# Folding W1's first two tiles before C0: a reordered first third of a two-layer adapter kernel

## The chip, the cores and the metric

One core of a Trainium2 chip runs the whole program. The metric is the device time of one execution in microseconds (us), lower is better. TensorE does the matmuls, VectorE (DVE) and ScalarE (ACT) split operands and empty PSUM, GpSimd (POOL) helps, and SyncE (SP) issues nearly all transfers between HBM and SBUF.

## The reference, cut to what matters

x is 8 batches of 256 tokens of 1024 features. Two residual layers follow each other, each a linear layer with adapters (`cond`) whose result only feeds a second linear map (`ffn`).

```
# layer 0: x = x + ffn0(cond0(x))
base   = x @ W0.T                              # W0: 1024 x 1024
cond0  = base + 2 * sum_e gate_e * (x @ A0_e) @ B0_e      # top-2 gates of 8, language bias
ffn0   = top1(cond0 @ route_w.T) * (cond0 @ A0f_e) @ Bw_e # 8 experts of rank 16
# layer 1: x = x + ffn1(cond1(x))
cond1  = x @ W1.T + b1 + 2 * (x @ lora_A[slot]) @ lora_B[slot]
ffn1   = cond1 @ Wb.T + b_base + 2 * (top-2 gates)*(cond1 @ A1_e) @ B1_e
```

Because `cond` is linear in x and only feeds linear maps, the kernel multiplies weights with weights first and the tokens afterwards. Three such products stand in the stretch that changes:

- **C0** (1024 x 136) = W0 folded with R0, the concatenation of route_w and A0f; **D0** is B0 folded with R0.
- **M** (1024 x 1160) = W1 folded with F, the concatenation of W_router, A1 and Wb. M goes on into the seven products of a Strassen scheme for all tokens.
- **FE** = the slots' lora_B folded with F.

## The kernel before, in words

Every f32 operand is split into a high part (an fp32r copy by ACT) and a low part (the rest, by DVE, line 789 via `lo`), and a product is three matmuls: high by high, high by low, low by high (`three`, lines 1239 to 1241). So each loaded operand costs one pass of ACT, then one of DVE, before TensorE may read it. C0 is the exception: two matmuls per step with R0's two parts side by side, 272 columns wide (`c0_step`, line 1246).

Each engine runs its program in the order written by hand; waits are on semaphores. A DMA queue belongs to SP, which also runs in order: a wait in it holds every later load.

TensorE's order before the main loop over the batches:

1. C0 from eight row tiles of W0 (128 matmuls of 272 columns), D0's fold (24 of 136).
2. FE in three column chunks of 240, 460 and 460 columns (`fe_steps`, 24 matmuls each), with `small0` (the tokens of the first two tiles times C0, 24 matmuls of 272) and its gates' turns between them.
3. The eight tiles of M, rows s = 0 to 7 (`m_chunk`; per row 24 matmuls of 240 and 48 of 460 columns). Row s uses PSUM banks 0 to 2 or 5 to 7 by turns. Behind row 0 stand the four groups of `ffn0`.
4. In the last two rows the chunk order is mixed; the bias matmul (`bias_part`, line 1380) stands behind row 6's second chunk.
5. The main loop `slot`, eight batches, which the change does not touch.

SP's order before: R0 and W0's row tiles, B0, the eight slots' lora_B, F in five pieces, A0, x, then W1's rows one at a time into one landing place (`load_w1`, each waits until the previous one is split), and behind row 1 the stores of FE to HBM (`fe_hi_dram`, `fe_lo_dram`).

DVE's pieces that the text speaks of: `gates0` (top-2 gates, ends in `hg`), `top1` (ends in `wh`), `b_times(k)` (six products for the bias row), `x1_add`, and per row of M the empty-out of PSUM (the loop over `add_ident`, `w1_split`, `lo`, `sub`, `lo_right`).

Of the kernel before, what the change touches and what calls it, by code (L numbers as in the profile page):

```python
# [5 lines left out]
P = 128  # L6
# [18 lines left out]
def adaln_ffn(nc, xT, lang_ids, slot_ids, W0, R0, A0, B0, Bw, W1, b1, lora_As, lora_Bs, F0, F1, F2, b_base, B1, out):  # L25

    C0C = ER + E + RC
# [6 lines left out]
    with ctx:  # L36
# [14 lines left out]
        C0lo, C0raw = twin("C0lo", [P, K, C0C])  # L51
        BwThi = sb("BwThi", [P, D], F32R)
# [175 lines left out]
        def m_count(s, c):  # L228
            return 3 * s + c + 1 if s < LAST else 3 * LAST + 2 * c + s - LAST + 1
# [41 lines left out]
        def by_batch(t):  # L271
            return t[:, :].rearrange("p (b k r) -> p k b r", b=NB, k=K)

        def k_first(t):
            return t[:, :].rearrange("p (k b r) -> p k b r", b=NB, k=K)
# [32 lines left out]
        def _(sp):  # L308
# [3 lines left out]
            def load_r0(g):  # L312
                load(r0_part(R0raw, g), R0[:, g * KH:(g + 1) * KH, :], r0_in[g])

            def load_f(i):
                c, k0, k1 = F_PARTS[i]
                load(f_part(i, 2), (F0, F1, F2)[c][k0 // KH if c else 0], f_raw_in[i])
# [4 lines left out]
            load_r0(0)  # L322
            for h in range(2):
                half = slice(h * D // 2, (h + 1) * D // 2)
                load(w0raw[0][:, half], W0[0:P, half], w0_in[0] if h else w0_half_in)
            load(w0raw[1][:, :], W0[P:2 * P, :], w0_in[1])
            load_r0(1)
            for j in range(2, K):
                load(w0raw[j][:, :], W0[j * P:(j + 1) * P, :], w0_in[j])
            load(b0raw[:, :], B0, b0_in)  # L330
            sp.wait_ge(ids_in, 32)
            for b in range(NB):
                slot = sp.value_load(ids[0:1, NB + b:NB + b + 1], min_val=0, max_val=lora_Bs.shape[0] - 1)
                load(w1raw[:, b * P:(b + 1) * P], lora_Bs[bass.ds(slot, 1), :, :].rearrange("s p c -> p (s c)"), bs_in)
            load_f(0)
            load(a0_part(C0raw), A0, a0_in)
            load(x_raw0[:, 0:D], xT[0, :, 0:D], x0_in[0])
            load_f(1)
            load_f(2)
            load(x_raw0[:, D:2 * D], xT[0, :, D:2 * D], x0_in[1])  # L340
            load_f(3)
            load_f(4)
            sp.wait_ge(bs_hi, 1)
            sp.wait_ge(bs_lo, 1)
            load_w1(0)
            load(BwTraw[:, :], Bw, bw_in)
            load(bcol[:, :], b1, bcol_in)
            load(x_raw1[:, 0:D], xT[1, :, 0:D], x2_in[0])
            sp.wait_ge(w1_hi, 1)
            sp.wait_ge(w1_lo, 1)  # L350
            load_w1(1)
# [34 lines left out]
            sp.wait_ge(w1_hi, K)  # L386
            sp.wait_ge(w1_lo, K)
# [69 lines left out]
        def _(gp):  # L457
# [10 lines left out]
            for g in range(2):  # L468
                gp.wait_ge(c0_hi, g + 1)
                c0 = slice(4 * g, 4 * g + 4)  # L470
                gp.tensor_tensor(C0lo[:, c0, ER + E:C0C], c0_sums[g], C0hi[:, c0, ER + E:C0C].bitcast(F32),
                                 ALU.subtract).then_inc(c0_lo, 1)
# [49 lines left out]
        def _(act):  # L522
# [5 lines left out]
            def r0_split(g):  # L528
                hi_half(r0_in[g], 16, r0_part(R0Thi, g), r0_part(R0raw, g), r0_hi)

            def f_split(i):
                hi_half(f_raw_in[i], 16, f_part(i, 0), f_part(i, 2), f_hi)

            def x_first(half):
                hi_half(x0_in[half], 16, xT_first[0][half][:, :], x_raw0[:, half * D:(half + 1) * D], xT_hi)

            def w1_split(s):
                hi_half(w1_in, 16 * (s + 1), ws_hi[s % 2][:, :], w1raw, w1_hi)

            r0_split(0)  # L540
            for h in range(2):
                hi_half(w0_in[0] if h else w0_half_in, 16, half_of(w0s_hi[0], h), half_of(w0raw[0], h), w0_hi)
            hi_half(w0_in[1], 16, w0s_hi[1][:, :], w0raw[1][:, :], w0_hi)
            r0_split(1)
            for j in range(2, K):
                hi_half(w0_in[j], 16, w0s_hi[j][:, :], w0raw[j][:, :], w0_hi)
            hi_half(b0_in, 16, b0hi[:, :], b0raw[:, :], b0_hi)
            act.wait_ge(w0_used, 2)
            hi_half(bs_in, 16 * NB, k_first(ws_hi[1]), by_batch(w1raw), bs_hi)

            def c0_half_part(g):
                hi_half(c0_done, g + 1, c0_sums[g], banks[:, 4 * g:4 * g + 4, RC:2 * RC], c0_half)

            def c0_part(g):
                hi_half(c0_sum, g + 1, C0hi[:, 4 * g:4 * g + 4, ER + E:C0C], c0_sums[g], c0_hi)

            c0_half_part(0)
            f_split(0)
            c0_part(0)
            c0_half_part(1)  # L560
            hi_half(a0_in, 16, a0_part(C0hi), a0_part(C0raw), a0_hi)
            c0_part(1)
            x_first(0)
            act.wait_ge(d0w_done, 1)
            act.activation(D0hi[:, :], p0[:, 0:RC], ACT.Copy, scale=2.0).then_inc(d0w_hi, 1)
# [83 lines left out]
            f_split(1)  # L649
            f_split(2)  # L650
            exp0(0)
            keep_fe(0)
            f_split(3)
            hgT_part(0)
            x_first(1)
            f_split(4)
            w1_split(0)
            whT_part(0, 0)
            keep_fe(1)
            hi_half(bw_in, 16, BwThi[:, :], BwTraw[:, :], bw_hi)  # L660
            exp0(1)
            keep_fe(2)
            hgT_part(1)
            w1_split(1)
            whT_part(1, 1)
            act.wait_ge(w1_lo, 2)
            act.wait_ge(fe_stored, 32)

# [3 lines left out]
            for s in range(LAST):  # L672
                par, row, p = s % 2, M_ROWS[s], s // 2
                act.wait_ge(m_ident, s + 1)
# [111 lines left out]
        def _(dve):  # L786
# [10 lines left out]
            def r0_split(g):  # L797
                lo_in(r0_hi, g + 1, r0_part(R0Tlo, g), r0_part(R0raw, g), r0_part(R0Thi, g), r0_lo)

            def f_split(i):  # L800
                lo_in(f_hi, i + 1, f_part(i, 1), f_part(i, 2), f_part(i, 0), f_lo)

            def x_first(half):
                dve.wait_ge(xT_hi, half + 1)
                lo(xT_first[1][half][:, :], x_raw0[:, half * D:(half + 1) * D], xT_first[0][half][:, :]).then_inc(xT_lo, 1)

            def w1_split(s):
                dve.wait_ge(w1_hi, s + 1)
                lo(ws_lo[s % 2][:, :], w1raw, ws_hi[s % 2][:, :]).then_inc(w1_lo, 1)
# [6 lines left out]
            r0_split(0)  # L816
            for h in range(2):
                lo_in(w0_hi, h + 1, half_of(w0s_lo[0], h), half_of(w0raw[0], h), half_of(w0s_hi[0], h), w0_lo)
            lo_in(w0_hi, 3, w0s_lo[1][:, :], w0raw[1][:, :], w0s_hi[1][:, :], w0_lo)
            r0_split(1)  # L820
            for j in range(2, K):
                lo_in(w0_hi, j + 2, w0s_lo[j][:, :], w0raw[j][:, :], w0s_hi[j][:, :], w0_lo)
# [786 lines left out]
```

## Time and profile before

| what | us |
|---|---|
| median of 3 runs | 466.69 (466.04 to 468.19) |
| the profiled execution's own time | 466.59 |
| its span in the profile, first to last instruction | 464.7 |
| TensorE busy in it | 447.0 (96%) |
| DVE busy | 306.9 (66%) |
| ACT busy | 151.0 (32%) |

Times in rows below are microseconds from the start of the span, so the execution's time is the span and 1.9 us around it. A timeline row gives start, duration, engine, line, operation, destination<-source, the shape, how many were merged, and in brackets how long the engine idled before it and what released it. Matmuls overlap, so a row's duration is longer than its distance to the next row; the distance is the pace. PEclk is the granted TensorE clock as a share of 2.4 GHz.

### The profile page before, as it was taken

What the parts mean: (1) busy time and instruction counts of PE and PEld (TensorE: products, weight loads), DVE (VectorE), ACT (ScalarE), POOL (GpSimd) and SP (SyncE); (2) the same over time, 40 slices, a digit from 0 to 9 for tenths busy, and PEclk for the clock granted to TensorE, in tenths of its full rate; (3) what the DMA queues carried; (4) which work ended last, traced back from release to release, by engine and by line L of the source; (5) the groups of instructions that cost most, each with busy time, mean ns of one, the idle gap of its engine ahead of it and who ended that gap; (6) DMA issues with size and microseconds to landing.
All of it is one profiled execution on the core that took longest, in us unless ns stands there. A gap on an engine that the chain in (4) does not pass through costs nothing.

```text
span 464.7 us, 7813 instructions
## 1 busy us (share of the span) xinstructions
PE 447.0 (96%) x2758; PEld 414.9 (89%) x2758; DVE 306.9 (66%) x911; ACT 151.0 (32%) x314; POOL 72.6 (16%) x62
## 2 busy tenths in 40 slices
PE   4988799999999999999999999999999999999997
PEld 4977799999988898889999999999999999999986
DVE  3897637574758688578557648738747755864852
ACT  4685212322222463234233224224323423321310
POOL 2040000000002412402402222120240230220110
PEclk9999899999999999999999999999999999999999
DMA  8993131111001101104103201211210310300302
GB/s 253 383 413 138 45 149 45 47 46 44 20 35 45 50 23 49 46 18 143 48 6 107 69 28 63 98 46 62 98 45 17 135 57 1 109 9 1 107 2 90
DMA packets 15151, 37.08 MB, mean 80 GB/s; under 512 B 2439, under 2 KB 7305, under 8 KB 15118
## 3 DMA queue, kind: packets, MB, share of 16 engines
q1 hardware_dynamic: 15022, 36.66, 22.7%
q8 instruction: 18, 0.29, 0.3%
q0 software_dynamic: 96, 0.00, 0.2%
q14 instruction: 15, 0.12, 0.1%
HBM read 27.07 MB, written 9.59 MB: 79 GB/s over the span
## 4 chain that ended last, share of the span: by engine, by line
PE 83%; DVE 12%; ACT 2%; issue 2%; DMA 1%; SPq 0%; DVEq 0%; ACTq 0%
PE banks L1239 25%; PE banks L1241 25%; PE banks L1240 25%; PE banks L1246 4%; DVE G L789 2%; DVE WbTlo L789 2%; PE banks L1471 2%; PE banks L1283 1%; DVE left L789 1%; DMA ws_lo_raw<-in_W_dram 1%; DVE ws_lo L789 1%; PE banks L1380 0%; DVE x_raw L973 0%; DVE G_raw L1086 0%; DVE w0s_lo L789 0%
## 5 line engine op out<-in xcount | busy, mean ns | idle before, releaser
L1239 PE MATMUL banks<-G,left 128*128 128x460 f32 x224 | 88.0, 393 | 0.0
L1240 PE MATMUL banks<-G,left 128*128 128x460 f32 x224 | 82.9, 370 | 0.0
L1241 PE MATMUL banks<-G,left 128*128 128x460 f32 x224 | 82.9, 370 | 0.0
L1239 PE MATMUL banks<-WbThi,ws_hi 128*128 128x460 f32 (+1 forms) x216 | 74.6, 345 | 4.3 <-DVE WbTlo L789 3.8
L474 POOL TENSOR_TENSOR xTlo<-x_raw,xThi 128x512 fp32r<-128x512 f32 x28 | 37.9, 1374 | 238.5 <-ACT xThi L572 114.6
L1241 PE MATMUL banks<-WbThi,ws_lo 128*128 128x460 f32 (+1 forms) x216 | 73.4, 340 | 0.0
L1240 PE MATMUL banks<-WbTlo,ws_hi 128*128 128x460 f32 (+1 forms) x216 | 73.1, 338 | 0.0
L526 ACT ACTIVATE left<-x_raw 128x512 fp32r<-128x512 f32 x64 | 38.7, 627 | 59.9 <-DVE x_raw L946 29.3
L1239 PEld LDWEIGHTS banks<-WbThi,ws_hi 128*128 128x128 f32 x216 | 40.6, 188 | 8.8 <-DVE WbTlo L789 4.9
L1239 PEld LDWEIGHTS banks<-G,left 128*128 128x128 f32 x224 | 42.4, 189 | 4.5 <-DVE wzTlo L789 0.3
L1241 PEld LDWEIGHTS banks<-G,left 128*128 128x128 f32 x224 | 42.1, 188 | 4.7
L1240 PEld LDWEIGHTS banks<-G,left 128*128 128x128 f32 x224 | 42.4, 189 | 2.6
L1240 PEld LDWEIGHTS banks<-WbTlo,ws_hi 128*128 128x128 f32 x216 | 40.8, 189 | 3.3
L1241 PEld LDWEIGHTS banks<-WbThi,ws_lo 128*128 128x128 f32 x216 | 40.7, 188 | 3.1
L946 DVE TENSOR_TENSOR x_raw<-banks,x_raw 128x512 f32<-128x512 f32 x32 | 22.1, 692 | 30.4 <-PE banks L1241 29.5
L977 DVE TENSOR_TENSOR ybuf<-banks,ybuf 128x460 f32<-128x460 f32 x48 | 29.6, 629 | 11.4 <-PE banks L1241 10.6
L1239 PE MATMUL banks<-Mdir,left 128*128 128x256 f32 x128 | 36.5, 285 | 0.2 <-DVE left L789 0.2
L474 POOL TENSOR_TENSOR left<-x_raw,left 128x512 fp32r<-128x512 f32 x16 | 20.7, 1312 | 98.8 <-DVE hg L858 74.0
L1240 PE MATMUL banks<-Mdir,left 128*128 128x256 f32 x128 | 35.9, 281 | 0.0
L1241 PE MATMUL banks<-Mdir,left 128*128 128x256 f32 x128 | 35.9, 281 | 0.0
L789 DVE SCALAR_TENSOR_TENSOR left<-x_raw,left 128x512 fp32r<-128x512 f32 x48 | 32.2, 686 | 2.7 <-ACT left L526 1.9
L1241 PE MATMUL banks<-C0hi,xTlo 128*128 128x272 f32 x112 | 32.3, 288 | 0.0
(178 smaller groups left out, 938.2 us busy)
## 6 DMA issues: line engine op xcount, KB each, us to landing
x_raw<-in_xT_dram SPq DMA_DIRECT2D x16, 512.0 KB, 3.8
out_dram<-ybuf SPq DMA_DIRECT2D x14, 512.0 KB, 2.7
x_raw<-in_W_dram SPq DMA_DIRECT2D x8, 512.0 KB, 3.3
WbTlo_raw<-in_F_dram SPq DMA_DIRECT2D x4, 920.0 KB, 12.8
w0s_lo_raw<-in_W_dram SPq DMA_DIRECT2D x6, 512.0 KB, 9.4
Fbuf<-fe_hi_dram SPq DMA_DIRECT2D x16, 64.0 KB
WbTlo_raw<-in_F_dram SPq DMA_DIRECT2D x1, 960.0 KB, 6.6
out_dram<-ybuf SPq DMA_DIRECT2D x3, 230.0 KB, 2.4
```

What stands on the lines that cost most here:

```text
L474: return gp.tensor_tensor(out_, a, b, ALU.subtract)
L526: act.activation(dst, src, ACT.Copy).then_inc(ready, 1)
L789: return dve.scalar_tensor_tensor(out=out_, in0=src, scalar=scale, in1=hi.bitcast(F32), op0=ALU.mult, op1=ALU.subtract)
L946: dve.tensor_tensor(raw_quarter(raw, g), by_half(bank), raw_quarter(raw, g), ALU.add).then_inc(x1_sum, 1)
L977: return dve.tensor_tensor(ybuf[tile][:, y0:y0 + n], bank, base, ALU.add).then_inc(ready, 1)
L1239: pe.matmul(out_, l[0], r[0], start=start, stop=False, **kw)
L1240: pe.matmul(out_, l[0], r[1], start=False, stop=False, **kw)
L1241: return pe.matmul(out_, l[1], r[0], start=False, stop=stop, **kw)
L1246: ins = pe.matmul(banks[:, k, 0:2 * RC], w, R0T[:, j, :], start=j == 0 and n == 0, stop=j == K - 1 and n == 1)
L1283: pe.transpose(dst, src, ident[:, :]).then_inc(done, 1)
L1471: pe.matmul(y, hsT[half][:, :], Fbuf[:, s], start=False, stop=True, skip_group_check=True)\
```

## The change

- TensorE's first work is sixteen transposes of the identity.
- It then folds rows 0 and 1 of M, from W1 pieces (five, `WF_PARTS`) and F pieces (eleven, `F_PARTS`) that SP loads first, in the order of use. FE and D0's fold follow.
- C0 comes after them. W0 is laid out in column tiles and streams through a ring of four buffers (`W0_RING`), so that each tile gives its own two column halves and finishes at once; SP loads a tile when its buffer is free. The sums are emptied in four pairs by ACT and DVE (POOL did the low part before).
- `small0`, the gates and the turns move in among rows 2 to 4 of M, `ffn0` into row 4, and DVE's `b_times` is spread otherwise. The slots' lora_B is laid out so that one DVE instruction splits it in place of eight.
- In SP's order the load of W1's row 3 stands behind the load of b_base, which waits for DVE's memset of `b_acc`.

SP, its list shown as it stands after:

```
+            load_wf(0)
+            load_f(0)
+            load_f(1)
+            load_wf(1)
+            load_wf(2)
+            load_wf(3)
+            load_f(2)
+            load_wf(4)
+            for i in range(3, 11):
+                load_f(i)
...
+            load(R0raw, R0, r0_in)
+            load_w0(0)
...
+            load_w1(2)
...
+            sp.wait_ge(m_done, m_count(0, 2))
+            load_w0(1)
+            sp.wait_ge(m_done, m_count(1, 2))
+            load_w0(2)
+            sp.wait_ge(fe_done, 3)
+            load_w0(3)
+            sp.wait_ge(d0w_done, 1)
+            load(BwTraw[:, :], Bw, bw_in)
+            sp.wait_ge(c0_used, 1)
+            load_w0(4)
             sp.wait_ge(fe_hi, 3)
             sp.wait_ge(fe_lo, 3)
             sp.dma_start(fe_hi_dram[0:P, :], fe_keep[0][:, :].bitcast(F32)).then_inc(fe_stored, 16)
             sp.dma_start(fe_lo_dram[0:P, :], fe_keep[1][:, :].bitcast(F32)).then_inc(fe_stored, 16)
+            for j in range(5, K):
+                sp.wait_ge(c0_used, j - 3)
+                load_w0(j)
             sp.wait_ge(acc_step, 1)
             load(b_acc[0:1, RC:MC], b_base.rearrange("(a o) -> a o", a=1), bbase_in)
-            for s in range(2, K):
-                sp.wait_ge(w1_hi, s)
-                sp.wait_ge(w1_lo, s)
+            for s in range(3, K):
+                sp.wait_ge(w1_hi, s - 2)
+                sp.wait_ge(w1_lo, s - 2)
                 load_w1(s)
```

ACT, from the last tile of W0 on:

```
+            w0_split(7)
+            act.wait_ge(c0_used, 5)
+            x_first(0)
+            c0_half_part(2)
+            w1_split(2)
+            c0_part(2)
+            c0_half_part(3)
+            c0_part(3)
+            act.wait_ge(c0_used, K - 1)
+            w1_split(3)
+            hi_half(bw_in, 16, BwThi[:, :], BwTraw[:, :], bw_hi)
+            act.wait_ge(fe_stored, 32)
+            x_first(1)
+            exp0(0)
+            hgT_part(0)
```

DVE, from the same place on:

```
+            x_first(0)
+            c0_add(2)
+            w1_split(2)
+            c0_part(2)
+            c0_add(3)
+            c0_part(3)
+            dve.wait_ge(fe_stored, 32)
+            dve.memset(b_acc[:, :], 0.0).then_inc(acc_step, 1)
+            w1_split(3)
+            lo_in(bw_hi, 1, BwTlo[:, :], BwTraw[:, :], BwThi[:, :], bw_lo)
+            x_first(1)
+            gates0(0, 0)
+            hgT_part(0)
...
+            b_times(0)
+            top1(0)
+            fold_rows(2)
+            whT_part(0, 0)
+            gates0(1, 0)
+            hgT_part(1)
+            b_times(1)
+            top1(1)
+            fold_rows(3)
+            whT_part(1, 1)
+            for g in range(2):
+                x1_add(0, g, x_raw0, X1W_FIRST[g])
+            b_times(2)
+            fold_rows(4)
...
+            fold_rows(5)
+            for k in range(6, K):
+                b_times(k)
```

TensorE:

```
+            pe.wait_ge(ident_ready, 1)
+            for _ in range(16):
+                pe.transpose(pt_h1, ident[:, :], ident[:, :])
+            pe.wait_ge(wf_lo, 1)
+            pe.wait_ge(f_lo, 1)
+            m_steps(0, 0, 0, 2)
...
+            for k in range(K):
+                pe.wait_ge(w0_lo, k + 1)
+                if k in (4, 6):
+                    pe.wait_ge(c0_sum, k // 2 - 1)
+                for j in range(K):
+                    for n, w in enumerate(split_of(W0_RING[k % 4][0], W0_RING[k % 4][1], j)):
+                        ins = pe.matmul(banks[:, C0_BANKS[k // 2] + k % 2, 0:2 * RC], w, R0T[:, j, :],
+                                        start=j == 0 and n == 0, stop=j == K - 1 and n == 1)
+                ins.then_inc(c0_used, 1)
+            pe.wait_ge(w1_lo, 1)
+            pe.wait_ge(fe_lo, 3)
+            m_chunk(0, 0)
             pe.wait_ge(a0_lo, 1)
+            pe.wait_ge(c0_lo, 4)
             pe.wait_ge(d0w_lo, 1)
             small0(0, first_tile(0), 1)
+            m_chunk(0, 1)
             pe.wait_ge(ident_ready, 1)
             turn_small(hg_ready, 1, pt_hg, hg[:, :], thg_done)
+            m_chunk(0, 2)
             add_lora0(0)
+            pe.wait_ge(w1_lo, 2)
+            m_chunk(1, 0)
             turn_small(wh_ready, 1, pt_wh, wh[:, :], twh_done)
             small0(1, first_tile(1), 2)
+            m_chunk(1, 1)
             turn_small(hg_ready, 2, pt_hg, hg[:, :], thg_done)
+            m_chunk(1, 2)
+            add_lora0(1)
...
+                if s == 4:
+                    turn_small(wh_ready, 2, pt_wh, wh[:, :], twh_done)
                 pe.wait_ge(m_lo, m_lo_at(s - 2, 3 + s % 2))
                 m_chunk(s % 2, 1)
+                if s == 4:
+                    pe.wait_ge(bw_lo, 1)
+                    pe.wait_ge(whT_lo, 2)
+                    ffn0(0, 0, X1W_FIRST[0])
+                    ffn0(0, 1, X1W_FIRST[1])
                 m_chunk(s % 2, 2)
```

`fold_rows(s)` is the old loop's body for one row: `add_ident`, `w1_split(s + 2)` where s > 1, and the empty-out. `wf_split`, `w0_split` and `c0_part` are the two-step splits (ACT high, DVE low) of the new pieces.

## Rows read from the trace of the kernel before

**Rows 1.** Windows: busy time of each engine, granted clock (PEclk), DMA share, GB/s.
```profile
7.06:12.04 4.98, 4.98 (x23) 4.98 (x23) 2.47 (x3) 2.78 (x3) 0.00 (x0) 1.00 0.95 324
13.31:25.47 12.16, 12.16 (x98) 12.15 (x97) 10.92 (x24) 8.17 (x8) 0.00 (x0) 1.00 1.07 384
30.00:35.00 5.00, 2.94 (x25) 2.78 (x24) 5.00 (x4) 3.88 (x4) 1.77 (x1) 1.00 1.02 417
45.00:50.00 5.00, 2.57 (x13) 2.02 (x13) 4.44 (x9) 1.32 (x2) 0.00 (x0) 1.00 0.00 0
50.00:55.00 5.00, 5.00 (x28) 4.90 (x27) 2.16 (x3) 1.67 (x3) 0.00 (x0) 0.66 0.33 105
59.00:61.00 2.00, 2.00 (x11) 1.76 (x10) 0.29 (x1) 1.22 (x2) 0.00 (x0) 1.00 1.01 411
```

**Rows 2.** TensorE's waits, 0 to 200 us: total, times, longest.
```profile
PE banks L1246 <- DVE ws_lo L789: 6.5, 1, 6.5
PE banks L1239 <- DVE WbTlo L789: 3.8, 3, 2.4
PE banks L1239 <- DVE D0lo L789: 2.1, 1, 2.1
```

**Rows 3.** TensorE's timeline: row 1 of M, row 2's start, the bias matmul.
```profile
72.21 0.27 PE L1239 MATMUL banks<-WbThi,ws_hi 128*128 128x240 f32 x1
...
74.91 0.37 PE L1239 MATMUL banks<-WbThi,ws_hi 128*128 128x460 f32 x1
...
84.98 0.27 PE L1239 MATMUL banks<-WbThi,ws_hi 128*128 128x240 f32 x1
...
147.12 0.50 PE L1380 MATMUL banks<-b_acc,ones 128*128 128x400 f32 x1
```

**Rows 4.** ACT's timeline: splits that begin when a load has landed.
```profile
3.70 0.66 ACT L526 ACTIVATE R0T<-R0T_raw 128x544 fp32r<-128x544 f32 x1 [1.69 <-DMA R0T_raw<-in_R_dram]
...
6.22 0.63 ACT L526 ACTIVATE ws_hi<-ws_lo_raw 128x512 fp32r<-128x512 f32 x1 [0.61 <-DMA ws_lo_raw<-in_W_dram]
...
9.79 0.66 ACT L526 ACTIVATE R0T<-R0T_raw 128x544 fp32r<-128x544 f32 x1 [1.25 <-DMA R0T_raw<-in_R_dram]
10.95 1.06 ACT L526 ACTIVATE w0s_hi<-w0s_lo_raw 128x1024 fp32r<-128x1024 f32 x1 [0.50 <-DMA w0s_lo_raw<-in_W_dram]
```

**Rows 5.** Transposes of gates (source view): duration min/median/max in ns.
```profile
L1283 PE MATMUL banks<-ident,hg x16: 270/272/328, 42.2 to 415.7; 128*128 128x128 f32 x16
```

**Rows 6.** DMA issues: KB each and median us from issue to landing.
```profile
x_raw<-in_W_dram SPq DMA_DIRECT2D x8, 512.0 KB, 3.3
```

**Rows 7.** DVE's timeline.
```profile
55.02 0.17 DVE L863 TENSOR_TENSOR lgc<-banks,bias 128x8 f32<-128x8 f32 x1 [1.44 <-PE banks L1241]
...
57.08 0.29 DVE L858 TENSOR_TENSOR hg<-banks,gc 128x128 f32<-128x128 f32 x1
...
61.91 0.17 DVE L914 COPY lgt<-banks 128x8 f32<-128x8 f32 x1 [2.18 <-PE banks L1241]
...
63.25 0.29 DVE L858 TENSOR_TENSOR wh<-banks,gt 128x128 f32<-128x128 f32 x1
...
65.36 1.02 DVE L1059 MEMSET b_acc<- 128x1160 f32 x1 [0.19 <-issue]
...
77.16 1.68 DVE L1071 SCALAR_TENSOR_TENSOR b_acc<-WbThi,bcol,b_acc 128x240 f32<-128x240 f32 x3
...
110.71 0.30 DVE L1082 TENSOR_TENSOR banks<-banks,ident 128x128 f32<-128x128 f32 x1 [5.81 <-PE banks L1241]
112.14 1.23 DVE L789 SCALAR_TENSOR_TENSOR ws_lo<-x_raw,ws_hi 128x1024 fp32r<-128x1024 f32 x1 [1.13 <-ACT ws_hi L526]
...
116.32 2.27 DVE L789 SCALAR_TENSOR_TENSOR G<-G_raw,G 128x460 fp32r<-128x460 f32 x4
```

**Rows 8.** SP's timeline: the load of b_base, then W1's rows.
```profile
66.41 0.32 SPq L310 DMA_DIRECT2D b_acc<-in_b_base_dram  x1
66.83 59.42 SPq L310 DMA_DIRECT2D x_raw<-in_W_dram  x6
```

More of the change, by code:

```diff
@@ L534, in x_first @@
             def x_first(half):
-                hi_half(x0_in[half], 16, xT_first[0][half][:, :], x_raw0[:, half * D:(half + 1) * D], xT_hi)
+                hi_half(x0_in[half], 16, xT_first[half][0][:, :], x_raw0[:, half * D:(half + 1) * D], xT_hi)
             def w1_split(s):
[L538 to L542, printed above, removed]
@@ L664, in _ @@
[L664 to L667, printed above, removed]
             def keep(out_, src, ready):
                 act.activation(out_, src, ACT.Copy).then_inc(ready, 1)
-            for s in range(LAST):
-                par, row, p = s % 2, M_ROWS[s], s // 2
+            wf_split(0)
+            f_split(0)
+            f_split(1)
+            wf_split(1)
+            wf_split(2)
+            wf_split(3)
+            f_split(2)
@@ new lines, in _ @@
+            wf_split(4)
+            for i in range(3, 11):
+                f_split(i)
+            hi_half(bs_in, 16 * NB, k_first(bs_hi_t), by_batch(bs_raw), bs_hi)
+            hi_half(r0_in, 16, R0Thi, R0raw, r0_hi)
+            act.wait_ge(bs_lo, 1)
+            w0_split(0)
+            hi_half(b0_in, 16, b0hi[:, :], b0raw[:, :], b0_hi)
+            hi_half(a0_in, 16, a0_part(C0hi), a0_part(C0raw), a0_hi)
+            act.wait_ge(m_ident, 1)
+            keep(direct(0, M_ROWS[0]), m_psum(0, 0), m_hi)
@@ new lines, in _ @@
+            keep_fe(0)
+            w0_split(2)
+            keep_fe(1)
+            keep_fe(2)
+            act.wait_ge(d0w_done, 1)
+            act.activation(D0hi[:, :], d0w, ACT.Copy, scale=2.0).then_inc(d0w_hi, 1)
+            w0_split(3)
+            c0_half_part(0)
+            w0_split(4)
+            c0_part(0)
+            w0_split(5)
+            c0_half_part(1)
+            w0_split(6)
+            c0_part(1)
+            w0_split(7)
+            act.wait_ge(c0_used, 5)
+            x_first(0)
@@ L1092, in lo_right, with fold_rows @@
                     ins.then_inc(ready, 1)
-            for s in range(LAST):
+            def fold_rows(s):
                 par, row, p = s % 2, M_ROWS[s], s // 2
                 add_ident(s)
-                w1_split(s + 2)
+                if s > 1:
+                    w1_split(s + 2)
                 dve.wait_ge(m_hi, m_hi_at(s, 1))
@@ L1115, in _ @@
                         lo_right(p, which, right_raw(p, which), g_lo)
-                for k in ((s,), (4, 5), (6, 7))[max(0, s - 3)]:
-                    b_times(k)
+            wf_split(0)
+            f_split(0)
+            f_split(1)
+            wf_split(1)
+            wf_split(2)
+            wf_split(3)
+            f_split(2)
+            wf_split(4)
+            for i in range(3, 11):
+                f_split(i)
+            lo_in(bs_hi, 1, k_first(bs_lo_t), by_batch(bs_raw), k_first(bs_hi_t), bs_lo)
@@ L1118, in _ @@
+            for g in range(2):
+                x1_add(0, g, x_raw0, X1W_FIRST[g])
+            b_times(2)
+            fold_rows(4)
+            for g in range(2, 4):
+                x1_add(0, g, x_raw0, X1W_FIRST[g])
+            for k in range(3, 6):
+                b_times(k)
+            fold_rows(5)
+            for k in range(6, K):
+                b_times(k)
             for s in (LAST, K - 1):
@@ L1312, in _, with first_tile, m_steps @@
-            pe.wait_ge(bs_lo, 1)
-            pe.wait_ge(f_lo, 1)
-            fe_steps(0, K)
+            def first_tile(t):
+                return lambda k: (rows(xT_first[t][0], k), rows(xT_first[t][1], k))
+            def m_steps(par, c, k0, k1):
+                for k in range(k0, k1):
+                    ins = three(m_psum(par, c), split_of(ws_hi[par], ws_lo[par], k),
+                                (Wb_of[c][0][:, k, :], Wb_of[c][1][:, k, :]), k == 0, k == K - 1)
+                if k1 == K:
+                    ins.then_inc(m_done, 1)
@@ new lines, in _ @@
+            pe.wait_ge(f_lo, 3)
+            m_steps(0, 0, 4, K)
+            pe.wait_ge(wf_lo, 5)
+            m_steps(1, 0, 4, K)
+            for k in range(0, K, 2):
+                pe.wait_ge(f_lo, 4 + k // 2)
+                for par in range(2):
+                    m_steps(par, 1, k, k + 2)
+            for k in range(0, K, 2):
+                pe.wait_ge(f_lo, 8 + k // 2)
+                m_steps(0, 2, k, k + 2)
+            m_chunk(1, 2)
+            pe.wait_ge(bs_lo, 1)
+            pe.wait_ge(m_lo, m_lo_at(0, 1))
@@ new lines, in _ @@
+            for c in range(3):
+                if c == 1:
+                    pe.wait_ge(m_lo, m_lo_at(0, 3))
+                for k in range(K):
+                    ins = three(m_psum(0, c), split_of(bs_hi_t, bs_lo_t, k),
+                                (Wb_of[c][0][:, k, :], Wb_of[c][1][:, k, :]), k == 0, k == K - 1)
+                ins.then_inc(fe_done, 1)
+            pe.wait_ge(b0_lo, 1)
+            pe.wait_ge(r0_lo, 1)
+            pe.wait_ge(m_lo, m_lo_at(1, 4))
+            for j in range(K):
+                ins = three(d0w, split_of(b0hi, b0lo, j), (R0Thi[:, j, :], R0Tlo[:, j, :]), j == 0, j == K - 1)
```

374 lines of the change are left out of this document (147 added, 227 removed).

## The prediction

> **What bounds the kernel now.** I read the windows first, to see where TensorE stands still or runs slowly; then its waits, for what ended them; then its timeline, for the pace of each kind of matmul; then the other engines' timelines and the DMA's, for the prices of what is moved. From 55 us on the windows show TensorE full, and the main loop is untouched, so the time changes by what reaches the bias matmul at 147.12 us [rows 3] sooner or later. Ahead of it TensorE stands still 6.5 us until the first operands are split, 2.1 us for the end of D0 and 3.8 us in three waits for F's low parts, the longest 2.4 us [rows 2]. Twice it is slow. In 7.06 to 12.04 us it began 22 matmuls of 272 columns (226 ns each; the window's 23 counts one cut off), later 96 in 12.16 us (127 ns) [rows 1]: half pace, although the profile writes a granted clock of 1.00 there. And after the 2.4 us wait the granted clock is 0.66 over 50 to 55 us, after 1.00 in the five before; at 1.2 GHz in part of it, that cost (1 - 0.66) x 5 = 1.7 us. The 2.1 us wait in 30 to 35 us was not followed by a fall [rows 1].
>
> So some 12 us of waiting and 4.7 us of slow clock (3.0 of its 6.0 us at the start, and 1.7) are what a better order could win. The question is what waits the new order has.
>
> **The change part by part.** Work for TensorE is the same but for the sixteen transposes. The paces: a row of M (72.21 to 84.98) takes 12.77 us, 2.70 for 24 matmuls of 240 columns (112 ns) and 10.07 for 48 of 460 (210 ns) [rows 3]; FE is one more such row; C0 and `small0` go at 127 ns.
>
> *Start.* The sixteen turns begin when the identity is there, near 1.6 us. At 0.27 us each as an upper bound [rows 5] they end by 6.0, at half that by 3.8. Landings I take from before by bytes: 0.28 MB in order at 3.70 us, 0.80 MB at 6.22, 1.61 at 9.79, 2.13 at 10.95 [rows 4]. The first F piece (0.38 MB with W1's first) so lands at 4.2; ACT 0.6, DVE 0.65, TensorE at 5.5 us, 1 us earlier than now. Until F's third piece is split it has 24 matmuls of 240 columns, about 200 ns each at half pace: done by 11. That third piece is the 1.77th MB, on hand at 10.15; ACT 1.0 and DVE 1.15 give 12.4 us. So TensorE waits over 1 us again, and whatever the turns save before it is swallowed here.
>
> *To the end of C0.* From 12.4: the other 24 of 240 (2.7), 96 of 460 (20.1), FE (12.8), D0 (24 at 112 ns, 2.7), five tiles of C0 (80 at 127 ns, 10.1): 60.9 us. The later F pieces arrive every 1.2 us and feed 2.5 us of matmuls each; the smaller pieces' extra issues on SP and extra passes cost nothing behind that. The slots' lora_B, R0, W0 tile 0, B0 and A0 land behind F by 27 us and are split by 29.5; FE needs them at 35: 5 us of cover, also if the strided split of lora_B takes twice its pass.
>
> *W0 tile 5.* SP issues it when tile 1 is used, at 54.9, but behind tile 4 (issued at 52.9) and FE's two stores of 0.59 MB. Tile 4 alone lands 3.3 us after issue [rows 6], at 56.2; 1.71 MB more at 411 GB/s [rows 1] make 4.2 us: 60.4. ACT 1.06, DVE 1.2: TensorE at 62.9. **A new stall of 2.0 us** (bounds: 0 if the tile passes the stores, 3.3 if the stores take twice their bytes' time). The last 48 matmuls of C0 end at 69.0. Before, the stores had no W0 behind them. Tile 4 itself is ready at 58.5, 0.3 us before its turn: hardly any cover. Emptying C0's earlier pairs hides behind the next tiles, and row 2's first chunk (2.7 us) hides the last pair from `small0`; that POOL gives its two passes to DVE costs DVE four short ones there.
>
> *The first gates.* `hg` needs `small0` and DVE. TensorE comes to its turn after 2.7 + 3.0 + 5.0 us, at 79.8. DVE and ACT empty C0's last pair (four passes of about 0.4 with the matmul's tail: 1.9) and set `b_acc` to zero (1.02 [rows 7]): 72.0. Only then may SP load b_base and, 0.42 us on [rows 8], W1's row 3; it lands 3.3 later [rows 6], at 75.7. In ACT's and DVE's order its split stands ahead of Bw's, x's second tile's and the gates: ACT 1.06, three DVE passes of 1.2 back to back (3.5) give 80.3, and `gates0` takes 2.35 (55.02 to the end of 57.08 [rows 7]). Ready at 82.9: **a new stall of 3.1 us**. Everything queued behind it on TensorE (rows 2 to 7) waits. Bounds: 1.8, if the row lands in 2.0 us, to 4.
>
> *The second `whT`.* From 83.1 TensorE has 5.0 + 0.3, row 3 with `small0` and small turns (12.8 + 3.0 + 0.6) and in row 4 two chunks and a turn (7.8): 112.7. DVE starts `top1(1)` when row 3 and `add_lora0(1)` end, at 105.0: 1.6 (61.91 to the end of 63.25), then all of `fold_rows(3)`, 7.9 (110.71 to the end of 116.32) [rows 7], then `whT_part`, 0.4: 114.9. **A new stall of 2.1 us** (1 to 3). Earlier the fold of a row had no turn behind it.
>
> *To the bias.* 24 matmuls of `ffn0` (2.8), 5.0, row 5 (12.8), 5.4 with 0.6 of the wait for the last `lo` that stands today too, 5.0: 146.7. DVE's last two `b_times` (3.2 each, from rows such as 77.16 [rows 7]) and the low parts of the last rows end near 145.9, so DVE covers by only 0.8 us: what delays it by more comes straight through. The gain with a full clock from 12.4 on is 147.12 - 146.7 = **0.4 us**.
>
> *Clock.* Two terms. At the start, now 6.0 us of matmuls run at half pace (6.48 to 12.5 us); 5.5 us of matmuls stand ahead of the wait for F's third piece, so 0.5 to 1 us more would run slowly behind it: +0.4 (bounds 0, and 2.4 if the 6.0 us count afresh from 12.4). Then the stalls: a wait of 2.4 us was followed by a fall that cost 1.7, one of 2.1 was not [rows 1, 2]. The 3.1 us one is beyond the first: +1.7. The two of 2.0 and 2.1 are nearest to the second: nothing, with 1.7 each as the other bound.
>
> A rule speaks against the turns. The row of before [rows 5] gives their length and cannot show what they do to the clock, as they stand singly there. The Trainium skill (TensorE: Matmul & The Clock Gate, Part 4: PE-mode transpose) says that the full clock does not engage for transposes. By that rule the +0.4 stands, as I take it; if turns do count, it goes, and the sum is 467.9 in place of 468.3. No run yet shows which.
>
> **Sum.** The profiled execution, 466.59 us, is 0.1 below the median. 466.59 - 0.4 + 0.4 + 1.7 = **468.3 us**.
>
> **Rivals.**
> 1. *The clock stays up in every stall.* For it: 2.1 us did not lower it. Against: 2.4 us did. 466.6 us.
> 2. *It falls at the 2.0 and 2.1 us stalls too.* For it: they are close to the one that did. 470.0 for one more fall, 471.7 for both.
> 3. *The slow start lasts 6.0 us afresh from 12.4.* For it: before, the pace rose after 6.0 unbroken us. Against: 5.5 us ran ahead. 468.3 + 2.0 = 470.3.
> 4. *The early loads run at full rate*: 0.28 MB at 3.70, then 411 GB/s, so F's third piece lands at 7.3 and TensorE never waits for it; the first burst at half pace ends near 10.3. That is 2.1 us off: 466.2. Against: before, only 1.33 MB came in the 6.1 us after 3.70 [rows 4], at 218 GB/s, with pieces of 2 KB per partition, and these are 1 to 2 KB. The Trainium skill (DMA: Bandwidth & Descriptors, Specifications) gives full rate from 512 B on, which would make this rival the forecast; the trace of before disagrees over its first 9 us.
> 5. *The first gates are not late* (the other side): W1's row 3 comes soon enough for `hg`. That takes away 3.1 us and the fall: 463.5. It decides once the chain from C0's end to `hg` (13.9 us) is 2.2 us shorter, for 468.3 - 2.2 - 1.7 = 464.4. For it: 3.3 us is a median, and DVE passes overlap a little. Against: three orders written by hand hold it (SP behind the memset, DVE behind C0, the gates behind three splits).
>
> **How the numbers follow.** Forecast 0.34 (467.3 to 469.3), rivals 0.15, 0.16, 0.10, 0.08, 0.17 in their order. What this kernel's measurement can tell from no change is about 0.5%, 2.3 us: 464.4 to 469.0. Faster: rival 5 and a third of rival 4, 0.20. Slower: rivals 2 and 3 and a third of the forecast, 0.37. Same: the rest, 0.43. The range leaves out about half of rival 5 below and the far half of the double fall above: 463.5 to 471.7.
>
> **What would show it.** Right: TensorE's first fold matmul near 5.5 us and a wait ended by F's third piece near 12; waits of about 2, 3 and 2 us before C0's sixth tile, the first `hg` turn and the first `ffn0`, at about 61, 80 and 113 us; a granted clock under 1.00 behind the second; the bias matmul near 148.4. Wrong: no wait at the `hg` turn, SP's load of W1's row 3 ahead of C0's end, or DVE's `b_times` holding the bias.

## The result and the profile after

| | before | after |
|---|---|---|
| median, us | 467.44 (466.04 to 468.20, 4 runs) | 473.85 (473.24 to 474.20, 4 runs) |
| profiled execution, us | 466.59 | 473.24 |
| its span, us | 464.7 | 471.4 |
| mean granted clock | 0.996 | 0.982 |

The ratio is 1.0139, 95% interval 1.0108 to 1.0170: the change makes the kernel 6.4 us slower. 468.3 was forecast, with a range up to 471.7. The bias matmul, which stood at 147.12 us [rows 3], now starts 6.3 us later, and behind it only 0.4 us more is lost (471.4 - 153.42 against 464.7 - 147.12), so all of it happens in the first third. TensorE's waits of the kernel after, 0 to 160 us, against [rows 2]:

```profile
PE banks L1342 <- DVE hg L901: 3.2, 1, 3.2
PE banks L1418 <- DVE ws_lo L843: 1.9, 1, 1.9
PE banks L1327 <- DVE whTlo L843: 1.9, 1, 1.9
PE banks L1327 <- DVE ws_lo L843: 1.8, 2, 1.3
PE banks L1372 <- POOL ident L489: 1.5, 1, 1.5
PE banks L1418 <- DVE w0s_lo L843: 1.0, 1, 1.0
PE banks L1327 <- DVE WbTlo L843: 0.9, 2, 0.6
```

The 6.5 us at the start, the 3.8 for F and the 2.1 for D0 are gone. In their place stand `hg` (3.2), W0's tile 5 (`ws_lo` at line 1418, 1.9), the second `whT` (1.9), W0's tile 4 (`w0s_lo`, 1.0) and short ones among the first pieces. They sum to 12.2 us, against 12.4 before; but the turns, 1.52 to 5.06 us, fill 3.5 us in which TensorE waited before, so 3.4 us more go by without a matmul of the work. The rest is in the windows (busy us of each engine, granted clock third from the end, then DMA share and GB/s):

```profile
5.00:10.00 5.00, 2.91 (x17) 2.44 (x17) 2.26 (x5) 1.87 (x4) 0.00 (x0) 0.82 0.85 292
10.00:15.00 5.00, 4.42 (x21) 4.17 (x21) 4.10 (x5) 4.14 (x5) 0.00 (x0) 0.50 1.03 416
15.00:20.00 5.00, 5.00 (x24) 4.79 (x23) 4.82 (x6) 4.19 (x5) 0.00 (x0) 0.66 1.02 364
...
60.00:65.00 5.00, 4.00 (x31) 3.63 (x29) 1.58 (x2) 1.75 (x3) 0.00 (x0) 1.00 1.03 415
65.00:70.00 5.00, 3.07 (x25) 3.00 (x25) 4.28 (x6) 4.67 (x8) 0.00 (x0) 1.00 0.18 70
...
85.00:90.00 5.00, 2.77 (x8) 2.50 (x9) 3.79 (x16) 0.57 (x2) 0.00 (x0) 0.67 0.06 20
...
120.00:125.00 5.00, 4.82 (x21) 4.54 (x22) 3.14 (x7) 0.00 (x0) 0.00 (x0) 0.66 0.00 0
```

The granted clock falls three times where it fell once before: from 8 to 18 us, behind `hg`, and behind the second `whT`. Behind W0's tile 5 (65 to 70 us) it stays at 1.00. TensorE's timeline shows the pace in each stretch (start, duration, line, output and inputs, the idle time before):

```profile
5.34 0.35 PE L1327 MATMUL banks<-WbThi,ws_hi 128*128 128x240 f32 x1 [0.29 <-DVE WbTlo L843]
5.53 0.28 PE L1328 MATMUL banks<-WbTlo,ws_hi 128*128 128x240 f32 x1
5.65 0.27 PE L1329 MATMUL banks<-WbThi,ws_lo 128*128 128x240 f32 x1
...
7.58 0.35 PE L1327 MATMUL banks<-WbThi,ws_hi 128*128 128x240 f32 x1 [1.32 <-DVE ws_lo L843]
...
12.60 0.54 PE L1327 MATMUL banks<-WbThi,ws_hi 128*128 128x240 f32 x1 [0.58 <-DVE WbTlo L843]
12.93 0.42 PE L1328 MATMUL banks<-WbTlo,ws_hi 128*128 128x240 f32 x1
13.14 0.41 PE L1329 MATMUL banks<-WbThi,ws_lo 128*128 128x240 f32 x1
...
87.22 0.45 PE L1342 MATMUL banks<-ident,hg 128*128 128x128 f32 x1 [3.18 <-DVE hg L901]
...
120.18 0.36 PE L1327 MATMUL banks<-whThi,BwThi 128*128 128x256 f32 x1 [1.91 <-DVE whTlo L843]
...
153.42 0.84 PE L1472 MATMUL banks<-b_acc,ones 128*128 128x400 f32 x2
```

The first fold matmuls start 0.11 to 0.12 us apart, which is the full pace of 112 ns; from the third F piece at 12.60 they start 0.21 us apart. The 24 matmuls behind that piece take 5.24 us, until 17.84, where 24 of 240 columns take 2.70 at the full clock. The loads of W0's tiles 4, 5 and 6 in 54 to 70 us (KB each, median us from issue to landing), and SP's order there:

```profile
ws_lo_raw<-in_W_dram SPq DMA_DIRECT2D x2, 512.0 KB, 6.4
...
w0s_lo_raw<-in_W_dram SPq DMA_DIRECT2D x1, 512.0 KB, 4.6
```

```profile
55.83 0.33 SPq L329 DMA_DIRECT2D w0s_lo_raw<-in_W_dram  x1
56.27 0.36 SPq L380 DMA_DIRECT2D fe_hi_dram<-fe_keep_hi  x1
56.67 0.43 SPq L381 DMA_DIRECT2D fe_lo_dram<-fe_keep_lo  x1
57.83 2.34 SPq L329 DMA_DIRECT2D ws_lo_raw<-in_W_dram  x2
...
76.38 0.30 SPq L329 DMA_DIRECT2D b_acc<-in_b_base_dram  x1
76.78 6.17 SPq L329 DMA_DIRECT2D x_raw<-in_W_dram  x2
```

Tile 4 takes 4.6 us where 3.3 was taken from [rows 6], tiles 5 and 6 take 6.4 in the median. W1's row 3 goes out at 76.78, behind the zeroing of `b_acc` (75.32 to 76.34), and ACT splits it at 80.23; the gates stand behind three splits on DVE, and `hg` is made at 86.79 to 87.08. That is the chain of 13.9 us as forecast, started later.

### The profile page after: what moved, and what is told of

Read it like the earlier page. It is cut to its first block, busy times and chain, and to the rows that moved or that the text cites. A ratio compares the mean times of both kernels' runs of the same rounds, so it can differ in the third digit from the quotient of the medians.

```text
span 471.4 us, 7865 instructions
## 1 busy us (share of the span) xinstructions
PE 453.6 (96%) x2774; PEld 420.8 (89%) x2774; DVE 308.6 (65%) x917; ACT 154.7 (33%) x325; POOL 67.5 (14%) x60
## 4 chain that ended last, share of the span: by engine, by line
PE 79%; DVE 12%; DMA 4%; ACT 2%; issue 2%; SPq 1%; DVEq 0%; ACTq 0%
PE banks L1327 25%; PE banks L1329 24%; PE banks L1328 24%; DVE G L843 3%; PE banks L1418 2%; PE banks L1563 2%; DMA ws_lo_raw<-in_W_dram 1%; DMA WbTlo_raw<-in_F_dram 1%; DVE ws_lo L843 1%; PE banks L1342 1%; ACT ws_hi L550 1%; DVE left L843 1%; DVE G_raw L1103 1%; DMA x_raw<-in_W_dram 1%; SPq L329 1%
## 5 line engine op out<-in xcount | busy, mean ns | idle before, releaser
L1329 PE MATMUL banks<-G,left 128*128 128x460 f32 x224 | 82.9, 370 | 0.0
L1327 PE MATMUL banks<-WbThi,ws_hi 128*128 128x460 f32 (+1 forms) x192 | 69.6, 362 | 3.1 <-DVE ws_lo L843 1.8
L1329 PE MATMUL banks<-WbThi,ws_lo 128*128 128x460 f32 (+1 forms) x192 | 67.7, 353 | 0.0
L1328 PE MATMUL banks<-WbTlo,ws_hi 128*128 128x460 f32 (+1 forms) x192 | 67.7, 353 | 0.0
L1327 PEld LDWEIGHTS banks<-WbThi,ws_hi 128*128 128x128 f32 x192 | 38.8, 202 | 7.1 <-issue 2.8
L1328 PEld LDWEIGHTS banks<-WbTlo,ws_hi 128*128 128x128 f32 x192 | 38.9, 202 | 2.9
L1329 PEld LDWEIGHTS banks<-WbThi,ws_lo 128*128 128x128 f32 x192 | 38.6, 201 | 2.8
```

What stands on the lines that cost most here:

```text
L1327: pe.matmul(out_, l[0], r[0], start=start, stop=False, **kw)
L1328: pe.matmul(out_, l[0], r[1], start=False, stop=False, **kw)
L1329: return pe.matmul(out_, l[1], r[0], start=False, stop=stop, **kw)
```

## The experiments

All are edits of the changed kernel. Ratios are against the kernel before, run beside them on the same chip; its median was 466.96 in the first four and 468.09 in the last four. The changed kernel was not run again beside them: its 473.85 stands beside 467.44, so a gain read as a difference of medians is uncertain by about 1 us.

The second to sixth edits leave the start as it is, and still it differs between the executions profiled: the first matmul of 460 columns, which stands right behind the 24 of F's third piece, starts at 17.84 us in the changed kernel and at 15.58 to 17.55 in those five. A part of each gain can come from there. In all four runs of the changed kernel the mean granted clock is 0.982; in the runs of the second to fourth edit it lies between 0.980 and 0.996, so the falls of the clock are not the same in every execution either.

**Without the sixteen turns.**

```diff
-            for _ in range(16):
-                pe.transpose(pt_h1, ident[:, :], ident[:, :])
```

> The changed kernel without its sixteen turns of the identity. It ran the first twelve fold matmuls 112 ns apart (full pace), fell to half pace near 8.2 us and stayed there until 17.9, which cost 2.5 us behind F's third piece at 12.6 us. Theory A: the turns raise the clock too early; matmuls then finish fast, TensorE stands idle between the loads, and the clock falls. Without turns the 24 early matmuls run 213 ns apart, fill the waits, and the pace rises about 6 us after the first of them, near 12: 2 to 2.5 us faster than the changed kernel, 471.5. Theory B: the turns do nothing to the clock, as the Trainium skill says (TensorE: Matmul & The Clock Gate, Part 4: PE-mode transpose); then the first matmuls run at 112 ns here too and the time stays at 473.8. Theory C: the slow spell comes from the waits for loads alone: first matmuls at 213 ns, rise again near 18, time within 0.5 us of 473.8.

Measured: 473.44 us (472.31 to 475.80, 4 runs), ratio 1.0154 (1.0108 to 1.0199); the same as with the turns. Its timeline tells what the turns do:

```profile
5.29 0.54 PE L1327 MATMUL banks<-WbThi,ws_hi 128*128 128x240 f32 x1 [5.29 <-DVE WbTlo L843]
...
14.35 0.34 PE L1329 MATMUL banks<-WbThi,ws_lo 128*128 128x240 f32 x1
14.52 0.27 PE L1327 MATMUL banks<-WbThi,ws_hi 128*128 128x240 f32 x1
14.63 0.28 PE L1328 MATMUL banks<-WbTlo,ws_hi 128*128 128x240 f32 x1
```

Without them the first 24 matmuls go at 0.21 us and the pace rises at 14.5, behind 9.2 us with two waits (the windows write a granted clock of 1.00 there, as they did at the start of the kernel before). With them it is full from the first fold matmul on in the changed kernel's profile; in four of the other seven profiles with turns it is full only from 6.1 to 6.5 us on, behind three to five matmuls at 0.21. So the turns do raise the clock, some 8 us sooner, and theory B is out. The gain is lost again in the waits before 12.6 us: here the first matmul of 460 columns starts at 16.54, 1.3 us sooner than with the turns. That is theory A's way and half its size; 0.6 of it goes into a longer wait for W0's tile 4 (1.62 against 1.00), and by the medians the time is the same, as C had it.

**W1's row 3 ahead of the wait for `b_acc`.**

```diff
+            sp.wait_ge(w1_hi, 1)
+            sp.wait_ge(w1_lo, 1)
+            load_w1(3)
             sp.wait_ge(acc_step, 1)
             load(b_acc[0:1, RC:MC], ...)
-            for s in range(3, K):
+            for s in range(4, K):
```

> SP's load of W1's row 3 put ahead of its wait for the memset of b_acc, nothing else. Theory A: the load by itself makes the first gates late. It lands about 4 us earlier (issued near 72.7 instead of 76.8 us), hg is there at 83, before TensorE's turn at 84; the wait of 3.2 us goes and with it the fall of the granted clock to 0.67 in 85 to 90 us, 1.7 us: 4.9 us faster, 469.0. Theory B: only the wait goes, and the slow spell comes from elsewhere: 3.2 us, 470.7. Theory C: the splits ahead of the gates move into C0's last emptying and the wait stays near 2 us: 1 to 2 us, 472.

Measured: 468.53 us (466.89 to 469.81, 10 runs), ratio 1.0031 (1.0014 to 1.0047). SP's timeline, then TensorE's waits:

```profile
71.86 0.33 SPq L329 DMA_DIRECT2D x_raw<-in_W_dram  x1
77.10 0.30 SPq L329 DMA_DIRECT2D b_acc<-in_b_base_dram  x1
```

```profile
PE banks L1330 <- DVE whTlo L846: 1.9, 1, 1.9
PE banks L1421 <- DVE ws_lo L846: 1.8, 1, 1.8
PE banks L1330 <- DVE ws_lo L846: 1.8, 1, 1.8
```

The row goes out 5 us ahead of b_base; no wait for `hg` stands among the longest or below them, and 5.3 us come back, where the wait of 3.2 and the fall behind it are 4.9: theory A, which gave 469.0. In this profile the second `whT` wait (1.91 us) has no fall behind it, and one of the same size, (0.24 + 0.10) x 5 = 1.7 us, stands behind W0's tile 5 (granted clock 0.76 in 65 to 70 us, 0.90 in 70 to 75); the two cancel.

**FE's stores behind W0's tiles 5 to 7.**

```diff
+            for j in range(5, K):
+                sp.wait_ge(c0_used, j - 3)
+                load_w0(j)
             sp.wait_ge(fe_hi, 3)
             ...
-            for j in range(5, K):
-                sp.wait_ge(c0_used, j - 3)
-                load_w0(j)
```

> The two stores of FE put behind the loads of W0's last tiles in SP's order, nothing else. Theory A: the stores hold tile 5 (1.9 us of wait) and slow tile 4 too (landing 4.6 us after its issue in place of 3.3, 1.0 us of wait): both waits go, 2.9 us faster, 470.9. Theory B: tile 4 is late because of the loads' own round trip (its buffer comes free only when tile 0 is used), the stores hold tile 5 alone: 1.9 us, 471.9. Theory C: both are bound by the ring of four buffers: within 0.5 us of 473.8.

Measured: 469.58 us (467.08 to 471.33, 10 runs), ratio 1.0051 (1.0025 to 1.0077); better than each theory gave. Its DMA view over 54 to 70 us:

```profile
ws_lo_raw<-in_W_dram SPq DMA_DIRECT2D x2, 512.0 KB, 4.3
...
w0s_lo_raw<-in_W_dram SPq DMA_DIRECT2D x1, 512.0 KB, 4.0
```

Tiles 5 and 6 take 4.3 us in place of 6.4, tile 4 takes 4.0 in place of 4.6. TensorE's wait for tile 4 shrinks to 0.4 us, the one for tile 5 to nothing, and `hg`'s is 2.8. That is 2.9 of the 4.3 us; the fold's first matmul of 460 columns also starts 0.85 sooner in this profile (16.99 against 17.84), which the edit doesn't touch. So the stores made both tiles late. Tile 4 was issued 0.44 us ahead of the first store in the changed kernel and still landed later for it; the 0.4 us left here are not the stores'.

**The second `whT` ahead of row 3's fold.**

```diff
-            fold_rows(3)
             whT_part(1, 1)
+            fold_rows(3)
```

ACT's half of it moves in the same way.

> whT_part(1, 1) put ahead of fold_rows(3) on DVE and ahead of row 3's part on ACT, nothing else. Theory A: the first ffn0 waits 1.9 us only because DVE empties a row of M first; that wait and the fall behind it (granted clock 0.66 in 120 to 125 us, 1.7 us) go: 3.6 us faster, 470.2. Theory B: the emptying of row 3, now begun 2.7 us later, makes a new wait in row 4 or 5 or at the bias matmul: 0 to 2 us faster. Theory C: a wait of 1.9 us does not lower the clock (one of 2.1 us did not in the kernel before), the fall has another cause: 1.9 us faster, 471.9.

Measured: 470.56 us (467.68 to 473.07, 10 runs), ratio 1.0072 (1.0043 to 1.0100): theory A. The windows have the granted clock at 1.00 where it was 0.66:

```profile
115.00:120.00 5.00, 5.00 (x31) 4.64 (x30) 4.72 (x9) 2.96 (x7) 0.00 (x0) 1.00 0.32 105
120.00:125.00 5.00, 5.00 (x26) 4.48 (x26) 5.00 (x11) 0.16 (x1) 0.00 (x0) 1.00 0.00 0
```

The wait is gone, and with it the fall: 3.3 us by the medians, where the wait of 1.91 and the fall of 1.7 are 3.6. The size is not settled by that. A part of theory B came too: the wait for `Mdir` in the last rows grows from 0.46 to 1.14 us. And in this profile the edit's gain is mixed with what it does not touch: the first matmul of 460 columns starts 1.8 us sooner (16.02), W0's tile 4 is waited for 0.7 us longer, and a fall stands behind tile 5 (0.66 in 65 to 70 us), where the changed kernel had none.

**All three edits together.**

> This kernel has all three of the single edits together: W1's row 3 loaded ahead of the wait on the first part of the carry, the fold's stores behind the loads of W0's tiles 5 to 7, and the second tile's wh split ahead of the copies of row 3. Each single edit gained against the changed kernel's 473.85 us: 5.3, 4.3 and 3.3. Theory A (three separate losses, so the gains add): 473.85 - 12.9 = 461.0 us, under the kernel before, with no wait of TensorE over 1 us between 50 and 140 us and the granted clock at 1.00 there. Theory B (a stall taken away early brings TensorE sooner to the next late operand, or a fall of the clock is shared by two of the stalls, so that the gains overlap): 464 to 466 us, with a wait left that none of the three singles shows. Theory C (SP, with the stores and row 3 moved, is late for the loads of W1's rows 4 and 5): 467 us or more.

Measured: 463.04 us (462.32 to 465.03, 6 runs), ratio 0.9902 (0.9871 to 0.9932): faster than the kernel before by 5 us, and 10.8 under the changed one where the singles sum to 12.9. Its waits up to 160 us:

```profile
PE banks L1329 <- DVE ws_lo L845: 2.1, 3, 1.3
PE banks L1374 <- POOL ident L492: 1.5, 1, 1.5
PE banks L1329 <- DVE Mdir L845: 1.1, 1, 1.1
PE banks L1329 <- DVE WbTlo L845: 1.0, 2, 0.7
PE banks L1420 <- DVE ws_lo L845: 0.4, 1, 0.4
```

The three stalls are gone, and the granted clock is 1.00 from 60 to 150 us. So A holds for the causes: three separate ones. One wait over 1 us is left against A's condition, 1.14 us for `Mdir`; it comes with the fold moved behind `whT` and was the same in that single. The size lies between A's 461.0 and B's 464 to 466. The profiles, one execution each, tell where the gap between 12.9 and 10.8 is not (us):

| | first matmul of 460 columns | bias matmul | between |
|---|---|---|---|
| changed kernel | 17.84 | 153.42 | 135.58 |
| row 3 early | 17.55 | 147.96 | 130.41 |
| stores late | 16.99 | 149.96 | 132.97 |
| `whT` first | 16.02 | 150.55 | 134.53 |
| all three | 17.16 | 142.80 | 125.64 |

Behind the start the singles gain 5.2, 2.6 and 1.1 us, 8.8 together, and the three edits 9.9, so there the gains do not overlap. Ahead of it the singles' profiles are 3.0 us sooner together and this one 0.7, which no edit made. C is out.

**TensorE kept busy while it waits for `hg`.**

```diff
+            for _ in range(24):
+                pe.transpose(pt_h1, ident[:, :], ident[:, :])
             turn_small(hg_ready, 1, pt_hg, hg[:, :], thg_done)
```

> The changed kernel with 24 turns of the identity ahead of the turn of hg, so that TensorE works through most of the time in which it waited for hg (3.18 us in the changed kernel's profile); hg itself stays late. Theory A (the fall of the clock behind the stall is a loss of its own, of 1.7 us, and goes when the engine is kept busy): 472.1 us, the granted clock at 1.00 from 85 to 95 us, hg turned at about the same time, 87.2. Theory B (the clock falls there for another reason than the idle time): 473.9 us, the granted clock at 0.67 from 85 to 90 as before. Theory C (the turns last beyond the time at which hg is ready, 24 at 221 ns): 475 us.

Measured: 470.77 us (467.99 to 472.05, 12 runs), ratio 1.0058 (1.0035 to 1.0080). TensorE's timeline:

```profile
81.89 2.78 PE L1432 MATMUL banks<-ident 128*128 128x128 f32 x24
85.16 0.33 PE L1342 MATMUL banks<-ident,hg 128*128 128x128 f32 x1 [0.49 <-DVE hg L901]
85.25 0.46 PE L1327 MATMUL banks<-WbThi,ws_hi 128*128 128x460 f32 x1
85.54 0.37 PE L1328 MATMUL banks<-WbTlo,ws_hi 128*128 128x460 f32 x1
```

`hg` is as late as ever (3.27 us behind the last matmul of the chunk), but the next matmuls run at full pace, and the granted clock from 85 to 90 is 1.00. The fall is a cost of its own, brought on by standing still: theory A. The 24 turns took 116 ns each at this clock, the 16 at the start of the changed kernel 221. The medians give 3.1 us where A gave 1.7; in this profile the fold also got under way 2.3 us sooner (15.58 against 17.84 us for the first matmul of 460 columns), and the second `whT` wait, 1.91 us again, had no fall behind it. Those two differ between executions, so the size of this gain is not settled by it.

**TensorE kept busy through the first pieces.**

```diff
             m_steps(0, 0, 0, 2)
+            fill(16)
             ...
             m_steps(0, 0, 2, 4)
+            fill(8)
             ...
             m_steps(1, 0, 0, 4)
+            fill(12)
```

`fill(n)` is n more turns of the identity.

> The changed kernel with 16, 8 and 12 further turns of the identity, in front of the waits for the fold's second, third and fourth pieces, so that TensorE is not idle between 5.3 and 12.6 us. Theory A (the clock falls at 8 us because of the short waits of 0.5 to 1.3 us, and the first 24 matmuls behind the third piece of F, at 218 ns instead of 112, are the price): 473.85 - 2.5 = 471.3 us, the granted clock at 1.00 from 8 to 18 us, and the first matmul of 460 columns at 15.5 to 16.0 us instead of 17.8. Theory B (the pieces arrive so late that the clock is of no matter there): 473.9 us. Theory C (the turns themselves are in the way): 475 us, the fold's pieces starting later than 7.6, 9.1 and 12.6 us.

Measured: 472.38 us (471.83 to 473.81, 6 runs), ratio 1.0096 (1.0067 to 1.0125). The windows:

```profile
5.00:10.00 5.00, 4.83 (x37) 4.46 (x37) 1.92 (x4) 1.36 (x4) 0.00 (x0) 1.00 0.71 231
10.00:15.00 5.00, 4.54 (x41) 4.33 (x40) 3.57 (x5) 3.95 (x5) 0.00 (x0) 1.00 1.04 417
15.00:20.00 5.00, 5.00 (x31) 4.58 (x31) 4.46 (x4) 3.35 (x4) 0.00 (x0) 1.00 1.03 387
```

The granted clock is 1.00 throughout (the first four fold matmuls still go at 0.21 us, all later ones at full pace), and the first matmul of 460 columns starts at 16.16 us, 1.7 sooner, though this profile's third piece came 0.8 later (13.39). So A's mechanism holds. Only 1.5 us reach the end by the medians, and 1.1 the bias matmul: the wait for W0's tile 4 grows from 1.0 to 1.8 and the one for `hg` from 3.2 to 4.0, with a longer fall of the clock behind it (0.50 in 85 to 90 us, 0.84 in 90 to 95: 3.3 us in place of 1.7), while the second `whT` wait has none.

**The three edits and the busy start.**

> The three edits together and the further turns at the start. Theory A (all losses separate): that of the three edits less the 1.0 to 2.5 us of the start, so 458.5 to 460 us if the three together give 461.0. Theory B (the pieces set the start, the clock does not): the same time as the three edits together, within 0.5 us.

Measured: 462.92 us (461.98 to 463.31, 6 runs), ratio 0.9884 (0.9857 to 0.9911): the time of the three edits alone, as B gave, but not for B's reason. The first matmul of 460 columns starts at 15.29 us against 17.16, and in the profile TensorE then waits 1.9 us for W0's tile 5 against 0.4, with a fall behind it:

```profile
62.98 0.39 PE L1426 MATMUL banks<-R0T,ws_hi 128*128 128x272 f32 x1 [1.94 <-DVE ws_lo L845]
```

```profile
65.00:70.00 5.00, 5.00 (x31) 5.00 (x30) 4.11 (x5) 3.47 (x5) 0.00 (x0) 0.71 0.09 35
```

In this execution the start is won and handed back: the longer wait costs 1.5 us and the fall up to 1.7 (0.95 in 60 to 65 us, 0.71 in 65 to 70). That tile's load took 5.6 us to land here and 4.3 with the three edits alone; what made it longer wasn't settled. The five other executions have a mean granted clock of 0.998 to 1.000 (0.995 in this one), so hardly any fall, and still take 461.98 to 463.28 us; what takes the gain there is not shown.

## Why the prediction was wrong, point by point

Slower by 6.4 us was measured, slower by 1.7 forecast. By the bias matmul, with the clock terms in it, 148.8 was forecast and 153.42 came, 4.6 us more:

- **Slow start** (+0.4, bounds 0 and 2.4): the step that failed. It counted 6.0 us of half-pace matmuls from 6.48 on, added up across the waits, and left 0.5 to 1 us of them behind F's third piece; if turns count, it left nothing. The landing was right (12.4 forecast, 12.60 measured), and so was the first fold matmul (5.5, 5.34). But the clock had risen with the turns and fell at 8.2 us, behind the waits of 0.29 and 1.32 us, so that the 24 matmuls behind the third piece took 5.24 us in place of 2.70: +2.5. The step had no term for a clock that is up and falls again in short waits. With TensorE kept busy there it stays at 1.00 and the 24 take 2.77. Rival 3 had the size (2.4), and its count afresh from 12.4 gives the rise at 18.4, where the profile has it near 18.3. But the five later profiles of the same start do not repeat it: the 24 matmuls take 2.8 to 4.2 us there, at the least hardly longer than at the full clock. So that this term came out near its upper bound is in part a matter of the execution.
- **The turns.** The prediction took its +0.4 by what the Trainium skill (TensorE: Matmul & The Clock Gate, Part 4: PE-mode transpose) says, that the full clock does not engage for transposes. The trace disagrees: sixteen turns raised the clock, since the matmuls behind them start 112 ns apart and without them 213. The other branch, that the term then goes, did not come either.
- **W0's tile 4** ("hardly any cover", 0.3 us, costed at nothing): 1.0 us, for the most part because of the stores, issued 0.44 us behind it: with them moved, the tile lands 4.0, 3.6 and 3.4 us after its issue in place of 4.6, and the wait is 0.4, none and none (stores late, all three, all three with the busy start). The prediction let the stores delay tile 5 alone. Tile 5's own term, 2.0, measured 1.9.
- **The first gates** (3.1 and a fall of 1.7): 3.18, and a clock of 0.67 in 85 to 90 us, (1 - 0.67) x 5 = 1.65. Right, shown by loading the row earlier.
- **The second `whT`** (2.1, no fall): 1.91, with a fall of (1 - 0.66) x 5 = 1.7. That is rival 2 in half, at 1.91 us where the row of before had none behind 2.1. Wrong on the fall; but the same wait of 1.9 us had none behind it in three of the six profiles that have it, so one row could not tell.
- **To the bias** (a gain of 0.4): the DVE cover of 0.8 us held (0.5 us of wait for `Mdir`, as before).
- **The strided split of lora_B** ("twice its pass"): 2.29 us against 1.06, and hidden, as said.

The misses, 2.1 + 1.0 + 1.7, make 4.8 of the 4.6 us; the small rest has the other sign. In the prediction's own sums, 62.9, 82.9 and 146.7 stand 0.2 to 0.3 us above what their terms add up to, and the bias matmul "near 148.4" should be 148.8 by its sum; neither decides anything. Rivals 1, 4 and 5 are out: the clock did not stay up, F's third piece came when forecast, and `hg` was late. That the new order can be worth its 0.4 and more is shown by the three edits: with the stalls gone, it beats the kernel before by 1.0% (0.9902).

## What to carry to other kernels

A wait on TensorE can have two prices: its length, and the clock behind it. When a change trades a long wait at the start for several of 1 to 3 us later, the sum of the waits can stay the same (12.4 and 12.2 us here) while the time rises. Ahead of such a change, take each new wait's operand back to its load: here three moves of one line each (a load ahead of an unrelated wait, stores behind loads that are due sooner, a small split ahead of a long fold) turned a loss of 6.4 us into a gain of 5.

## What the runs showed of the hardware that was not expected

Whether the clock falls behind a wait of about 2 us is not told by the wait's length alone. In the profiles of the changed kernel and its eight variants, between 50 and 125 us:

| idle time of TensorE | stalls | of them with a granted clock under 1.00 behind them |
|---|---|---|
| 2.80 to 3.97 us (`hg`) | 5 | 5 |
| 1.83 to 1.97 us (tile 5, `whT`) | 13 | 6 |
| 0.42 to 1.76 us (tile 4) | 7 | 0 |

The same wait for `whT`, 1.91 us, had a fall behind it in the changed kernel and none with W1's row 3 loaded early. A term for the clock behind a wait of about 2 us is therefore a chance, near one half in these runs, and not a yes or no read off one row. In the first 13 us, where waits stand close together, shorter ones were enough: in the changed kernel the clock fell at 8.2 us behind waits of 0.29 and 1.32 us.
